# Issuing PV of two attention steps together, and whole projections by a fixed list, in a one-core attention and channel-mix kernel

## What is computed

```python
q, k, v = (layernorm(x) @ w.T for w in (w_q, w_k, w_v))       # 16 heads of 16
weights = softmax(q @ k.T * 0.25)                             # 1024 x 1024 for each batch and head
x = x + layernorm((weights @ v) @ w_o.T)
n = layernorm(x)                                              # channel mix over halves of a batch
prev = n shifted by one row (zeros ahead of row 0)
xr, xk = mu_r * n + (1 - mu_r) * prev, mu_k * n + (1 - mu_k) * prev
x = x + layernorm(sigmoid(xr @ W_r.T) * (relu(xk @ W_k.T) ** 2 @ W_v.T))
```

## Time and profile before

| | us |
|---|---|
| median of 3 runs | 1449.12 (1447.71 to 1449.77) |
| profiled execution | 1448.0, span 1446.2 |
| busy: PE / ACT / DVE / POOL | 1354.5 / 1015.3 / 858.2 / 299.2 |
| first exponential starts at | 45.9 |
| last exponential ends at | 1395.4 |

### The profile page before, as it was taken

The page is one execution under the profiler, slowest core; times in us unless marked ns, Lnnn a source line. Parts: engine busy times, 40 slices in busy tenths (PEclk is TensorE's granted clock), DMA queues, the critical chain, the costliest instruction groups (busy, mean ns, idle before and its releaser), DMA issues.

```text
span 1446.2 us, 21872 instructions
## 1 busy us (share of the span) xinstructions
PE 1354.5 (94%) x8916; PEld 607.8 (42%) x8916; DVE 858.2 (59%) x1738; ACT 1015.3 (70%) x1080; POOL 299.2 (21%) x366
## 2 busy tenths in 40 slices
PE   3889999999999999999999999999999999999974
PEld 2433454444443444344443444444444444433433
DVE  5442575567647585565755666466754647463747
ACT  2558767777677677777777776776777777788751
POOL 7100211213111221212112222111311121211221
PEclk9999999999999999999999999999999999999996
DMA  3562534215232345115441152422442054301010
GB/s 131 143 161 86 113 64 103 59 60 116 63 86 59 108 82 106 43 44 132 88 103 49 56 130 45 103 59 75 101 94 61 23 131 88 75 2 30 1 30 15
DMA packets 61311, 112.79 MB, mean 78 GB/s; under 512 B 6400, under 2 KB 31232, under 8 KB 61184
## 3 DMA queue, kind: packets, MB, share of 16 engines
q1 hardware_dynamic: 61184, 111.05, 31.9%
HBM read 69.08 MB, written 41.94 MB: 77 GB/s over the span
## 4 chain that ended last, share of the span: by engine, by line
PE 79%; ACT 12%; DVE 7%; issue 1%; POOL 0%; DMA 0%
PE O L410 28%; PE M L193 25%; PE S L391 21%; ACT PT L398 11%; PE M L465 2%; PE M L442 2%; DVE A L561 1%; PE M L235 1%; DVE scratch L560 1%; DVE C L188 1%; DVE xA L227 1%; DVE scratch L576 0%; DVE B L188 0%; DVE p L264 0%; DVE Z L188 0%
## 5 line engine op out<-in xcount | busy, mean ns | idle before, releaser
L398 ACT ACTIVATE PT<-S 128x1024 f32<-128x1024 f32 x1024 | 983.9, 1024 | 318.1 <-PE S L391 318.1
L410 PE MATMUL O<-PT,V 128*17 128x512 f32 x4096 | 541.0, 600 | 0.0
L391 PE MATMUL S<-QS,KS 50*128 50x512 f32 x2048 | 417.3, 465 | 34.7 <-ACT PT L398 30.2
L391 PEld LDWEIGHTS S<-QS,KS 50*128 50x128 f32 x2048 | 169.8, 184 | 295.6 <-ACT PT L398 211.6
L193 PE MATMUL M<-WH,B 128*128 128x256 f32 x768 | 165.9, 298 | 14.0 <-DVE B L565 6.4
L193 PEld LDWEIGHTS M<-WH,B 128*128 128x128 f32 x768 | 127.6, 193 | 97.0 <-issue 39.5
L505 POOL TENSOR_SCALAR veh<-mvh 128x2 f32<-128x2 f32 x96 | 21.2, 221 | 583.3 <-DVE mvh L503 582.9
L410 PEld LDWEIGHTS O<-PT,V 128*17 128x17 f32 x4096 | 68.0, 95 | 160.1 <-issue 159.9
L193 PE MATMUL M<-WL,B 128*128 128x256 f32 x384 | 109.4, 285 | 0.0
L193 PE MATMUL M<-xnT,WH 128*128 128x512 f32 x256 | 92.8, 445 | 9.8 <-DVE xnT L243 9.8
L637 DVE RECIPROCAL Z<-Z 128x512 f32<-128x512 f32 x30 | 100.6, 3353 | 1.0
(11 more groups left out here) (101 smaller groups left out, 1263.6 us busy)
## 6 DMA issues: line engine op xcount, KB each, us to landing
scr<-p SPq DMA_DIRECT2D x124, 256.0 KB
QS<-scr SPq DMA_DIRECT2D x60, 256.0 KB, 5.0
KS<-scr SPq DMA_DIRECT2D x60, 256.0 KB, 7.0
QS<-scr SPq DMA_DIRECT2D x68, 128.0 KB, 4.3
KS<-scr SPq DMA_DIRECT2D x68, 128.0 KB, 7.3
xA<-x_dram SPq DMA_DIRECT2D x16, 512.0 KB, 7.1
xB<-x_dram SPq DMA_DIRECT2D x16, 512.0 KB, 7.6
out_dram<-xB SPq DMA_DIRECT2D x15, 512.0 KB, 3.5
```

The lines of the kernel that those rows point to most:

```text
L391: fn = lambda e, p=p, a=a, rows=rows: e.matmul(PS[p][:, a, :], KS[qd][rows, p, kt * 128:kt * 128 + 128], QS[qd][rows, p, hf * 512:hf * 512 ...
L398: e_fn = lambda e, p=p: e.activation(PT[i % 2][:, 2 * p:2 * p + 2, :], PS[p][:, :, :], ACT.Exp, scale=SCALE)
L410: fn = lambda e, j=j: e.matmul(PO[g % 2][32 * j:32 * j + 17, :], V[b % 2][:, kt, 4 * qd + j, :], PT[i % 2][:, j, :], start=(kt == 0), stop ...
```

## The change

PV is emitted for two steps together, in the odd ones: S(s even), other work, S(s odd), PV of both. The planner with its costs and rate is gone. In its place the lists have 32 cells, separated by "|", and cell s is emitted whole in step s. The words with matmuls stand in the even cells alone, so between the two steps' scores, and no projection is cut in pieces; ot of the half's own groups is in the lists as N0 to N2. What yields REST is kept in `resting` and goes on in the next step. PT has four buffers and the exponential waits for PV of four steps earlier. The spreads come after steps 12, 20 and 27, for batch 0 after step 6, and the DMA scratch size of the build is set to 256.

```diff
-STEPS, RATE = 29.00, 0.750
...
-        PT = [sb(f"PT{i}", [128, 4, 512]) for i in range(2)]
+        PT = [sb(f"PT{i}", [128, 4, 512]) for i in range(4)]
...
-                exp_of[i, p] = act.op(e_fn, s_of[i, p], pv_of.get(i - 2))
+                exp_of[i, p] = act.op(e_fn, s_of[i, p], pv_of.get(i - 4))
...
-        EVEN = """P0 P1 P2 Oot3 . P3 P4 Oct0 . Oct1 P5 . Oy0 Oy1 . . . Ox0 Ox1 P6 . Oz0 . Oz1 Oxr0 Oxr1 Oxk1 . P7
-            . . Oxk0 . Or0 . Or1 . Ok0 . Ok1 Osig0 . Oact0 . Osig1 Oact1 . . . . Ov0 Ov1 . Oout0 Oout1"""
-        ODD = """P0 . Oot3 . P1 Oct0 . . . P2 Oct1 . P3 Oy0 Oy1 P4 . Ox0 Ox1 . Oz0 . Oz1 P5 Oxr0 . Oxr1 Oxk1
-            Oxk0 . . . Or0 Osig0 . Or1 P6 Osig1 . Ok0 . P7 Oact0 . Ok1 Oact1 . . . Ov0 Oout0 Ov1 . Oout1"""
-        FIRST = """B6 B7 B0 B1 B2 B3 P0 P1 P2 . P3 P4 P5 P6 P7"""
-        NEW = (15, 20, 30)
+
+
+
+        EVEN = """Oot3 P0 P1 P2 | | Oct0 Oct1 P3 | | P4 | | Oy0 | | Oy1 | Ox0 | P5 | Ox1 | N0 | | Oz0 Oz1 | Oxr0 |
+            P6 Oxr1 | Oxk1 Oxk0 | Or0 | | Or1 N1 | Osig0 | Ok0 | Osig1 | Ok1 | Oact0 | P7 | Oact1 | Ov0 N2 | |
+            Ov1 Oout0 | Oout1"""
+        ODD = """Oot3 P0 | | Oct0 Oct1 P1 | | P2 | | Oy0 | | Oy1 | Ox0 | P3 | Ox1 | P4 N0 | | Oz0 Oz1 P7 | Oxr0 |
+            P5 Oxr1 | Oxk1 Oxk0 | Or0 | | Or1 N1 | Osig0 | Ok0 | Osig1 | Ok1 | Oact0 | P6 | Oact1 | Ov0 N2 | |
+            Ov1 Oout0 | Oout1"""
+        FIRST = """B6 B7 | | B0 B1 | | B2 B3 | | P0 P1 P2 | | P3 P4 | | P5 | | P6 N0 | | P7 | | | | | | N1 | | | | | |
+            | | N2 | | |"""
         LN1_AT = (2, 6, 13, 16)
-        SPREAD_AT = (16, 24, 27)
-
-        COST = {"t": .43, "q": .65, "k": .65, "v": .65, "ot": .43, "ct": .43, "y": .65, "z": .43, "r": .65}
+        SPREAD_AT = (12, 20, 27)
...
+            if word[0] == "N":
+                return o_turn(u, int(word[1:]))
             if word[0] in "PB":
                 b = u // 2 + 1 if word[0] == "P" else 0
                 name = AHEAD[u % 2 if word[0] == "P" else 1][int(word[1:])]
-                return (ahead(b, name), COST[name[0]], 1 if name[0] == "t" else 2) if b < B else None
-            if word == ".":
-                return rest, 0, 1
-            at = u - 1
-            kind = word[1:-1]
-            pieces = 2 if kind in ("y", "k", "r", "v") else 1
-            return (kinds[kind](at, int(word[-1])), COST.get(kind, 0), pieces) if at >= 0 else None
-
-        def rest():
-            yield REST
+                return ahead(b, name) if b < B else None
+            return kinds[word[1:-1]](u - 1, int(word[-1])) if u > 0 else None
...
+        resting = []
+
+        def until_rest(work):
+
+            for said in work or ():
+                if said == REST:
+                    resting.append(work)
+                    return
...
-            todo = [w for w in (part(u, word) for word in (FIRST if u == 0 else (EVEN, ODD)[hf]).split()) if w is not None]
-            rate = max((sum(c * n for _, c, n in todo) + 3 * COST["ot"]) / STEPS, RATE)
-            pieces = in_pieces(todo)
-            cost, spent = next(pieces, None), 0.0
+            cells = [cell.split() for cell in (FIRST if u == 0 else (EVEN, ODD)[hf]).split("|")]
             for s in range(32):
                 i = 32 * u + s
                 if i + 1 < len(steps):
                     scores(i + 1)
-                values(i)
+                if s % 2:
+                    values(i - 1)
+                    values(i)
                 if s == 0 and u > 0:
                     load_xb(u - 1)
-                if s in NEW:
-                    o_turn(u, NEW.index(s))()
-                    spent += COST["ot"]
-                if cost == REST:
-                    cost = next(pieces, None)
-                while cost is not None and (cost <= 0 or spent + cost / 2 <= rate * (s + 1) or s == 31):
-                    if cost == REST and s < 31:
-                        break
-                    spent += max(cost, 0.0)
-                    cost = next(pieces, None)
+                again, resting[:] = resting[:], []
+                for work in again:
+                    until_rest(work)
+                for word in cells[s]:
+                    fn = part(u, word)
+                    if fn is not None:
+                        until_rest(fn())
                 if u == 0 and 3 <= s < 7:
                     split_weights([W_NAMES[s]])
-                if (u, s) == (0, 12):
+                if (u, s) == (0, 6):
                     spread(0, 2)
...
+        while resting:
+            until_rest(resting.pop(0))
...
-    nc = _bacc.Bacc("TRN2", target_bir_lowering=False, num_devices=1)
+    nc = _bacc.Bacc("TRN2", target_bir_lowering=False, num_devices=1, dynamic_dma_scratch_size=256)
```

More of the change, by code:

```diff
@@ L397, in scores @@
                         s_of[i, p] = pe.op(fn)
-                e_fn = lambda e, p=p: e.activation(PT[i % 2][:, 2 * p:2 * p + 2, :], PS[p][:, :, :], ACT.Exp,
+                e_fn = lambda e, p=p: e.activation(PT[i % 4][:, 2 * p:2 * p + 2, :], PS[p][:, :, :], ACT.Exp,
                                                    scale=SCALE)
-                exp_of[i, p] = act.op(e_fn, s_of[i, p], pv_of.get(i - 2))
+                exp_of[i, p] = act.op(e_fn, s_of[i, p], pv_of.get(i - 4))
                 last_exp[p] = exp_of[i, p]
@@ L410, in values @@
                 fn = lambda e, j=j: e.matmul(PO[g % 2][32 * j:32 * j + 17, :], V[b % 2][:, kt, 4 * qd + j, :],
-                                             PT[i % 2][:, j, :], start=(kt == 0), stop=(kt == 7))
+                                             PT[i % 4][:, j, :], start=(kt == 0), stop=(kt == 7))
                 if j < 3:
@@ L726, in together @@
                 live = [g for g in live if next(g, DONE) is not DONE]
-        def in_pieces(todo):
-            for fn, cost, pieces in todo:
-                yield cost
-                for rest in fn() or ():
-                    yield REST if rest else cost
         def split_weights(names):
@@ L844, in sandwich_kernel @@
         for words in LAST.split():
-            together([part(2 * B, word)[0] for word in words.split("+")])
+            together([part(2 * B, word) for word in words.split("+")])
         block = ctx.enter_context(nc.Block())
```

## The result

The changed kernel takes **1495.18 us** (median of 4 runs, 1494.08 to 1496.95), the kernel before 1449.01: a ratio of 1.0321, with a 95% interval of 1.0303 to 1.0339. It is 3.2% slower; the forecast was 1473, in a range of 1400 to 1512. The sign and the range held, the size was half of what came. The profiled execution spans 1493.4 us against 1446.2, so 47.2 us are to be found.

The account below looks back on a forecast made before the run. TensorE's order of work was taken as the bound, ScalarE's exponentials a second limit. From 1448.0 profiled: +4 (halves 2 to 13), +6 (last two), +2 (first two), +12 (clock) = 1472, or 1473 as median; range 1400 to 1512.

Parts of the forecast that it names:

- The two bounds of a pair: Per pair of steps: PE work with PV of both in 1.86 us (4.80 with a projection), and ACT's minimum of 4.84.
- the floor: ACT's exponential latency with two PSUM tiles for scores: at least 4.84 us a pair, 77.4 us for 16 pairs.
- Rival 4: Second step's PV weight load not hidden, two steps take 2 x 0.98: 26 us more, 1499 in all; chance 0.03.
- The wait at the even half's start: Four transpositions in one cell: PE waits 5.2 us over a projection's time for DVE's evictions, then 1.1 two cells on.
- The wait for xr: Or0 (s = 18) waits for xr from DVE and POOL: 2.3 us in even halves, 1.7 in odd ones.
- Or0's turn would be at 2 x 4.84: Or0 due 9.7 us after Oz0 starts, but xr's low part on POOL ready at 11.95: 2.3 us of waiting.
- the couples: Six even-odd pairs of halves (2 to 13): 171.2 us each against 170.4, +4 in all, before +12 for the clock.
- The clock: TensorE's clock falls behind the four-transposition cell in each of six even halves, 2 us each: +12 (bounds 0 and 17).
- For the gaps of 1.7 to 2.3 I take no fall: No clock fall at the shorter waits, as for xr; one each would cost up to 15 x 2 us.
- The first two halves: 91 + 84.4 us against 173.6, +2, with about 6 us of P2 waiting on P0's eviction behind DVE's queue.
- The last two halves: ACT's minimum stands although cells are empty: 159.8 us against 153.4, +6.
- Behind the last exponential: The stretch after attention ends: no term in the sum, taken as unchanged at 50.8 us.

Follow-up runs that it names:

- Experiment 1: The changed kernel with the four transpositions at the start of even halves spread over three cells, P3 to P5 moved later: 1455.26 us.
- Experiment 2: The changed kernel with both xr mixing words put ahead of the eviction of P6 (P5 in odd halves): 1453.86 us.
- experiment 6: The changed kernel with 12 unused matmuls between P0 and P1 in even halves, keeping PE busy during its wait: 1482.85 us.
- experiment 9: The kernel with repaired lists (1384.97 us), with the next step's scores split around the first PV in pairs without a projection: 1374.03 us.
- Experiment 8: The kernel with repaired lists (1384.97 us), plus a list for the last half that brings its final projections and output norms forward: 1383.28 us.
- experiment 10: The kernel with repaired lists, with the next step's scores split around the first PV in all 256 pairs: 1433.66 us.

## Why the prediction was right, point by point

**The two bounds of a pair: right.** PV of two steps in 1.85 us (402.18 to 404.03) where 1.86 was worked out; a pair on the floor 4.79 for 4.84. It is 1.84 to 1.85 in 239 of the 256 pairs; of the other 17, 15 overlap a stretch at the lower clock, and behind the other two PE stands still. Rival 4 falls with that: unhidden, the second step's load would have shown 1.96 or more. The Trainium skill (TensorE: Matmul & The Clock Gate, The mechanism) has a rule that LDWEIGHTS overlaps running matmuls only where the row group differs, by which PV of two steps would not run together; the same section also says that a load into the background weight buffer is pulled ahead. The trace disagrees with the first and fits the second, and the measurement decides.

**The wait at the even half's start: right.** 3.28 + 0.67 us for the 3.75 + 0.95 of the sum, third transposition 1.07 for 1.1. Experiment 1 shows that this cell is the cause. The order of DVE's queue (copy, normalization, statistics, POOL, normalization, eviction) was read from the printed order with durations from before, and none of its steps was off by more than half a microsecond.

**The wait for xr: right in size, but not all of it.** 2.14 and 1.80 us for 2.3 and 1.7. The step "Or0's turn would be at 2 x 4.84" followed DVE and POOL to PE and stopped there. It did not follow the same late DVE work to ACT, where line 627 wants Z and the exponentials stand behind it: 8.4 us instead of 7.1 in the pair of Or0, in the six odd halves 1 to 11. Odd halves came to 85.5 where 84.4 stood, and to 84.4 in half 13, which lacks that wait. Experiment 2, in which xr comes earlier, takes that pair to 5.4. This is the whole miss of the couples (+22 for +16).

**The clock: mechanism right, its size too small.** The term "six even halves, 2 us each" measured 3 in experiment 6: I let part of the slow stretch lie over the waiting, but in five of six it lies over the work behind. The first two pairs of an even half took 10.5 and 7.9 us in the changed kernel, and 9.7 and 5.9 in experiment 6 with the clock up; the sum had 4.84 + 5.2 = 10.0 and 4.84 + 1.1 = 5.9 before the clock. So the waits stand within 0.4 us and the clock is 2.8. That the even half was 88.7 on average for 88.8 is in part luck: without the clock it is 85.9 in experiment 6 where the sum had 86.8, and the clock took 0.8 more than its term. "For the gaps of 1.7 to 2.3 I take no fall" was wrong in seven of fourteen halves, at little cost. ("Before, this happens once within attention" leaves out a second slow stretch of the trace of before, 3.4 us at 48.3.)

**The first two halves: the largest miss.** 183.9 for 175.4. The first half took 97.8 for 91, the second, an odd one, 86.1 for 84.4. The step "ahead of P0's eviction, on which P2 waits: about 6 us, and the clock with it" had the wait and its size (6.21 us), but not two others ahead of it. DVE's and PE's timeline of the changed kernel:

```profile
64.15 0.69 DVE L187 CAST p<-M 128x512 fp32r<-128x512 f32 x1 [2.62 <-DMA scr<-p]
...
69.21 1.11 PE L234 MATMUL M<-ident,xA 128*128 128x128 f32 x4 [2.92 <-DVE p L263]
...
76.54 1.12 PE L234 MATMUL M<-ident,xA 128*128 128x128 f32 x4 [6.21 <-DVE xnT L242]
...
69.06:82.70 13.64, 7.28 (x30) 2.85 (x32) 10.27 (x26) 1.94 (x2) 1.76 (x2) 0.50 0.76 165
```

The evictions into p wait for the stores that read p's earlier contents; I had asked PE's and DVE's queues what was late but never when p itself comes free. DVE stood 2.62 us here and 2.17 at the next one, PE 2.92 before its second transposition, and the clock was at 0.50 for 13.6 us.

**The last two halves.** 163.3 for 159.8. The floor is as it stood; the window above has a clock of 0.96 where the earlier trace rows have 1.00, in four slow stretches of 3.4 us that the sum did not hold. One follows the wait for xr (1.74 us). In the 10 us ahead of each of the other three PE waits only for exponentials, in pairs on the floor, 0.89 us at most. In experiment 9, where another step's PV fills such waits and the one for xr is gone, these halves have no slow stretch. So it is not only one long gap after which the clock falls, and here the sum had nothing for it.

**Behind the last exponential: not foreseen.** I gave it no term, since no word of it changed. Timeline of the changed kernel at the end of attention:

```profile
1442.06 0.42 DVE L454 TENSOR_TENSOR CC<-M,rec 128x256 f32<-128x256 f32 x1
...
1442.54 1.97 PE L464 MATMUL M<-ident,CC 128*128 128x128 f32 x8 [3.95 <-DVE CC L454]
```

and the same place before:

```profile
1398.77 1.09 PE L465 MATMUL M<-ident,CC 128*128 128x128 f32 x8 [0.81 <-DVE CC L455]
```

It is the queue of the even half's start once more: the last group's eviction stands behind the output norm of half 14, 3.95 us instead of 0.81. That is 3.1 of the 7.2 us. For the rest the windows show two things and no run divides them: the clock falls 5.8 us behind the last exponential instead of 11.4 (0.67 on average over the stretch, 0.71 before), and DVE has 3.2 us more to do in it (39.0 for 35.8). Experiment 8, which brings these words forward, takes 4.3 of the 7.2 away. The reasoning of the even half's start, carried to the end, would have given the wait.

In sum: between forecast and result are 22 us, of which 8.5 are the first two halves, 7.2 the tail, 6.2 the odd halves of the couples, 3.5 the last two halves, less 2.4 for an earlier first exponential (the rest is rounding and the distance of the profiled execution from the median). Two of the four, the odd halves and the tail's wait, have one cause: a lateness on DVE that I followed to one waiter and not to the next. In the first half it is a tile that a store still reads, in the last two the clock. What stays open: why one wait of 1.80 us is followed by a slow stretch and another of the same length is not, and what the clock's part in the tail is.

## What to carry to other kernels

A fixed order that makes the bound engine's pure work smaller also makes it wait whenever a cell wants a buffer that the evicting engine frees late: before pricing the saving, write out that engine's queue for each cell, with what it itself waits for (a store that still reads the tile), and follow the lateness to the end of the program. Here the same pairing gave +3.2% with one order of the words and -4.3% with another; a list of where each word goes deserves as much care as the idea that it serves. Two parts that each cost 11 to 13% alone stand at +3% together and gain once the order is mended, so an experiment that does one part alone judges the part, not the idea.

## What the runs showed of the hardware

- Idle time of TensorE cost twice here. With the wait of 3.28 us the granted clock was 0.50 for 6.8 us (410.40 to 417.20 in half 4), in all six even halves; after waits of 1.74 to 2.15 us it was so for 3.4 us in seven of fourteen halves, and not at all in the others. In the last two halves it fell three times for 3.4 us where no wait was longer than 0.89 us. In the 6.8 us some 3 us are lost, shown by experiment 6, in which matmuls of no use in the gap keep the clock at 1.00.
- PV of two steps runs as one stream: 1.85 us for two, 0.98 for one, though both use all 128 rows.
- Splitting a pair's scores, which adds one change from scores to PV and one back, costs PE 0.29 us a pair (5.09 against 4.80 in experiment 10), though no data is waited for.
- The two PSUM tiles between scores and exponentials set a floor of 4.8 us a pair that stands with four buffers behind the exponential (4.79, 1387.09 to 1391.88), and that one PV put between the two tiles' scores lowers (experiment 9: 4.45).
